# Permutation builds tied to a counted gather in the first pass of a two-layer graph network

## The reference

```python
def gcn_conv(x, edge_index, edge_weight, W, b, n_nodes):
    # self-loops added; norm = dinv[row] * ew * dinv[col]
    h = x @ W
    msg = h[row] * norm[:, None]
    out = segment_sum(msg, col, num_segments=n_nodes)
    return out + b

h = maximum(layernorm(x), 0)
x = x + log_softmax(gcn_conv(relu(gcn_conv(h, ..., W1, b1)), ..., W2, b2))
h = maximum(layernorm(x), 0)
msg  = relu(h[src] + edge_attr @ We + be)
aggr = segment_sum(msg, dst)
x = x + relu(batchnorm(relu((h + aggr) @ W1 + b1) @ W2 + b2))
```

## Time and profile before

| | us |
|---|---|
| median of 3 runs | 5606.34 |
| lowest and highest | 5599.08, 5607.18 |
| the profiled execution | 5616.2 |
| its span, first to last instruction | 5614.4 |
| TensorE busy | 4328.9 |
| VectorE busy | 3689.5 |
| GpSimd busy | 3768.6 |
| the first pass, first to last gather of the loop and its tail | about 270 to 2432 |

### The profile page before, as it was taken

One profiled execution on the slowest core, in us unless ns is written; L12 is line 12 of the kernel. 1 busy time (PEld: TensorE's weight loads), 2 busy tenths in 40 slices (PEclk: granted clock), 3 DMA queues, 4 the chain that ended last, 5 costly groups with the idle time before them and its releaser, 6 DMA issues.

```text
span 5614.4 us, 116632 instructions
## 1 busy us (share of the span) xinstructions
PE 4328.9 (77%) x29893; PEld 3358.6 (60%) x29894; DVE 3689.5 (66%) x10748; ACT 1292.0 (23%) x4287; POOL 3768.6 (67%) x3554
## 2 busy tenths in 40 slices
PE   4566666666666666668999999996699999999995
PEld 4444444444444444456777777775577777777773
DVE  3466666665666666647888888886666666666662
ACT  5111111111111111142111111113433333332223
POOL 2377777777777777737777777775666665666663
PEclk6577787777778787859999999996899999999997
DMA  2122222222222222212222222223232322222224
GB/s 54 37 47 46 50 47 47 48 47 48 46 48 46 49 48 49 46 52 52 52 51 51 51 51 51 51 48 111 65 70 65 70 68 66 70 62 67 63 59 109
DMA packets 239972, 316.92 MB, mean 56 GB/s; under 512 B 69263, under 2 KB 175178, under 8 KB 239545
## 3 DMA queue, kind: packets, MB, share of 16 engines
q0 software_dynamic: 111232, 170.85, 15.6%
q1 hardware_dynamic: 128688, 145.48, 8.9%
HBM read 276.92 MB, written 39.15 MB: 56 GB/s over the span
## 4 chain that ended last, share of the span: by engine, by line
PE 60%; DVE 13%; POOL 11%; issue 10%; DVEq 2%; ACT 2%; DMA 1%; POOLq 0%; ACTq 0%; SPq 0%
PE psum L1222 26%; PE psum L1142 15%; POOL rows_g L658 11%; PE psum L1165 7%; PE psum L1129 3%; DVE x_tab L1662 2%; PE psum L1086 2%; PE psum L1150 2%; PE psum L1154 1%; DVE x_tab L1657 1%; DVEq L432 1%; PE psum L1214 1%; PE psum L1289 1%; DMA rows_g<-table,idx 1%; DVE rows_g L1619 1%
## 5 line engine op out<-in xcount | busy, mean ns | idle before, releaser
L658 POOL DMA_INDIRECT rows_g<-table,idx x3476 | 3605.6, 1037 | 1547.3 <-issue 1011.3
L1222 PE MATMUL psum<-x_tab 125*128 x8512 | 1148.9, 289 | 83.9 <-issue 46.2
L1142 PE MATMUL psum<-hot,rows_g 128*96 128x128 f32 x7512 | 1077.4, 297 | 143.5 <-DMA rows_g<-table,idx 70.7
L1142 PEld LDWEIGHTS psum<-hot,rows_g 128*96 128x96 f32 x7512 | 980.8, 181 | 236.4 <-issue 145.8
L1222 PEld LDWEIGHTS psum<-x_tab 125*128 125x128 bf16 x8512 | 827.3, 97 | 393.9 <-issue 135.0
L1165 PE MATMUL psum<-x_tab 128*104 128x512 bf16 x2432 | 614.5, 403 | 534.4 <-DVE x_tab L1662 526.3
L1582 DVE TENSOR_TENSOR acc<-acc,psum 96x128 f32 x1173 | 328.8, 280 | 962.9 <-PE psum L1142 945.2
L791 ACT ACTIVATE attr<-edge 128x12 f32 (+1 forms) x1173 | 243.5, 211 | 2806.3 <-PE psum L1142 2805.6
L1165 PEld LDWEIGHTS psum<-x_tab 128*104 128x104 bf16 x2432 | 303.1, 133 | 780.6 <-ACT x_tab L848 321.9
L1573 DVE TENSOR_SCALAR hot<-iota,attr 128x128 f32<-128x128 f32 x2504 | 686.4, 356 | 7.3 <-ACT acc L785 4.8
L1619 DVE TENSOR_REDUCE rows_g<-psum 128x384 f32<-128x1152 f32 x304 | 412.3, 1356 | 341.2 <-PE psum L1222 336.9
(11 more groups left out here) (255 smaller groups left out, 3692.3 us busy)
## 6 DMA issues: line engine op xcount, KB each, us to landing
rows_g<-table,idx POOLq DMA_INDIRECT x3476, 2.5
x_tab<-sorted_keys SPq DMA_DIRECT2D x304, 125.0 KB
x_more<-in_edge_attr_dram SPq DMA_DIRECT2D x238, 64.0 KB
sorted_attr<-x_tab SPq DMA_DIRECT2D x38, 384.0 KB
x_more<-sorted_attr SPq DMA_DIRECT2D x152, 96.0 KB
table<-x_tab SPq DMA_DIRECT2D x13, 840.0 KB
x_tab<-in_edge_attr_dram SPq DMA_DIRECT2D x38, 256.0 KB, 2.8
x_tab<-in_x_dram SPq DMA_DIRECT2D x2, 4200.0 KB
```

What stands on the lines that cost most here:

```text
L658: pool.indirect_dma_start(out=rows_g[u][0:np_, g * F:(g + 1) * F], out_offset=None, in_=table[p], in_offset=bass.IndirectOffsetOnAxis(ap=i ...
L1142: last = pe.matmul(ps_agg[t.b], rows_g[t.u][0:t.np_, g * F:(g + 1) * F], hot[t.h][0:t.np_, g, :], start=g == 0, stop=g == G - 1)
L1222: last = pe.matmul(ps_sel[c], mask[i % 2][j][:, c * P:(c + 1) * P], tab3[:, j:J - KB + 1 + j, :, :][:, bass.ds(w[c], 1), :, :].rearrange(" ...
```

## The change

In the first pass GpSimd increments `fast.issue` ahead of every gather, so four times a step; in the other passes once a step, as before. Each build waits for that semaphore beside its old wait: build m of step k of iteration it waits for the count (it*U + k)*G + LEAD + m + 1 with LEAD = 16. In steps 3 to 7, those with three builds, VectorE's list is written in another order: build, addition, one hot, build, two hots, build, one hot. For that `build_hot` takes the columns that it is to build. Step 2 keeps its order and gets the wait.

```diff
+    LEAD = 16
...
             def gather(ring, p, s, u, np_, got):
                 pool.wait_ge(ring.staged, p * NS + s + 1)
-                pool.sem_inc(ring.issue, 1)
                 for g in range(G):
+                    if g == 0 or p == 0 and ring is fast:
+                        pool.sem_inc(ring.issue, 1)
                     pool.indirect_dma_start(
...
-            def build_hot(p, t):
+            def build_hot(p, t, columns=range(G)):
                 n = p * NS + t.s
                 np_ = t.np_
-                dve.wait_ge(fast.staged, n + 1)
-                dve.wait_ge(fast.agg, n + 1 + U - H)
+                if columns[0] == 0:
+                    dve.wait_ge(fast.staged, n + 1)
+                    dve.wait_ge(fast.agg, n + 1 + U - H)
...
-                    for g in range(G):
+                    for g in columns:
...
-                last.then_inc(fast.hot, 1)
+                if columns[-1] == G - 1:
+                    last.then_inc(fast.hot, 1)
...
-            def sort_perm(it, c):
+            def sort_perm(it, c, k, m):
                 dve.wait_ge(s_permd, SC * it + c + 1)
+                dve.wait_ge(fast.issue, (it * U + k) * G + LEAD + m + 1)
                 dve.tensor_scalar(perm[c % 3], iota_h, rank[:, c:c + 1], None, ALU.is_equal).then_inc(s_perm, 1)
...
+                        cs = PERM_AT.get(k, ())
+                        if len(cs) == 3:
+                            sort_perm(it, cs[0], k, 0)
+                            add_window(0, Step(it, k), w[k] * AL)
+                            build_hot(0, Step(it, k + LA), (0,))
+                            sort_perm(it, cs[1], k, 1)
+                            build_hot(0, Step(it, k + LA), (1, 2))
+                            sort_perm(it, cs[2], k, 2)
+                            build_hot(0, Step(it, k + LA), (3,))
+                            continue
                         build_hot(0, Step(it, k + LA))
...
-                        for c in PERM_AT.get(k, ()):
-                            sort_perm(it, c)
+                        for c in cs:
+                            sort_perm(it, c, k, 0)
```

## The result

The changed kernel takes 5660.07 us (median of 4 runs, 5658.26 to 5663.74), the kernel before 5605.26 us in the same comparison (5599.08 to 5607.18). The ratio is 1.0097 with a 95% interval from 1.0078 to 1.0116: slower by 54.8 us. The forecast was 5644 with a range of 5555 to 5705. The profiled execution of the changed kernel took 5663.74 us, 47.5 more than the profiled one of before.

A forecast was written before the change was run, and what follows sets the result against it. GpSimd's gathers were taken to bound the first pass. Stalls of 5.5 + 0.3 us an iteration against 4.8 gave +1.0, over 38 iterations +38 us on 5606: 5644 us, range 5555 to 5705.

The forecast's parts named there:

- What bounds the pass: First pass: it lasts as long as GpSimd's gathers; mean gather to rise from 1.076 to about 1.10 us, gap unchanged at 0.30.
- Signals and the wait: First pass: three more semaphore increments a step cost nothing; builds reach their waits 3.5 to 7.6 us late, so none holds.
- Rival B: First pass: waits hold, each build starts 0.2 us ahead of a gather, stretching it to 1.38 us; +80 us, 5686; chance 0.10.
- rival C: First pass: waits hold, but builds end before a gather's needs and stalls vanish; about -100 us, 5506; chance 0.03.
- The size: First pass: stalls beside builds go from 4.8 us an iteration to 5.5 + 0.3, so +1.0 us, +38 us over 38 iterations.
- The walk: Gathers followed through one step of the new order: three stalls, 0.24, 0.55 and 0.30 us, 1.09 a step, 5.5 an iteration.
- What it put at 0.55 us: GpSimd, let in at build 2's end, stops again inside build 3, which ends 1.17 us after build 2: 0.55 us lost.
- what it put at 0.30: GpSimd stops again in the next step's build 1, which ends 0.92 us after build 3: 0.30 us lost.
- the first hit: Build 2 nearly always hits a gather's stop, holding it for 0.27 us on average: 0.24 us a step.
- my upper bound of +3.6: Two hots and a build hold GpSimd as one, as three builds do: 8.4 us an iteration against 4.8, +3.6.
- The two stops: A long VectorE instruction can hold a gather at two points only, 0.13 and 0.79 us into it.
- The step of additions: First pass: the time from one VectorE addition to the next falls from 4.82 to 4.6 us.

The follow-up runs named there:

- `LEAD` 28: The changed kernel with LEAD = 28 in place of 16, so each signal comes three steps later; 5629.99 us, ratio 1.0026 to the kernel before.

## Why the prediction was right, and where it was not

*What bounds the pass.* Right. The idle time of GpSimd stayed at 475 us and all that moved was the mean gather, forecast at about 1.10 and measured at 1.104 us. Passes 2 and 3 kept their length within 0.4 us.

*Signals and the wait.* Right. The signals cost nothing, and the order alone gives the ratio of the whole change (1.0081 against 1.0097, overlapping). The builds come late to their signals, by 5 to 12 us in the mean and never by less than 2.7; I had worked out 3.5 to 7.6. That a signal runs twelve gathers ahead is confirmed by `LEAD` 28, with which waits begin to hold. Rival B's price of an aligned build (gather of 1.38 us) was met within 0.04 us there; rival C's shield didn't appear.

*The size.* The forecast was +1.0 us an iteration, and the stalls went from 5.27 to 6.34 us (mean of iterations 3 to 38), +1.07. Over 38 iterations that is 41 of the 42 us in the pass. The last 5 us of the profiled difference were in no term, and the medians differ by 7 us more than the profiled executions do.

*The walk.* Its mechanism stands: GpSimd slips in at the end of a build with a hot behind it and stops again inside the next build. What it put at 0.55 us (the next build 1.17 behind) is 2.12 - 0.94 - 0.63 = 0.55 in the gathers of 2.1 us (0.63 is the wait for build 2, from 0.13 us on), if they were let in at that build's end; what it put at 0.30 (0.92 behind) is 0.22 to 0.23. Two of its terms were mis-sized, and they cancelled. It took five of the 0.55 and four of the 0.30 an iteration, and the trace has 2.0 and 2.9. It took 0.24 us for the first hit, a mean over all phases, and the gathers that are stopped twice had waited 0.63 and 0.48 us at their first stop. So the sum of +1.0 came out by luck in part. The walk also spread the three stalls over gathers of 1.2 to 1.6 us. But first and second stop belong to one gather, so they add up in it: 165 gathers of 1.6 to 2.2 us carry 160 of the 248.8 us, 4.2 of 6.5 us an iteration, and those of 1.2 to 1.6 became fewer (176 to 146). That two hots and a build hold GpSimd as one, the mechanism of my upper bound of +3.6, is neither shown nor excluded; at every step it doesn't happen. Gathers over 2.4 us, which were to tell of it, are gone but for one of 2.98.

*The two stops.* I put them at 0.13 and 0.79 us into a gather, counted back from its end. That takes for granted that a release costs nothing. In the run with two builds ahead of the hots, 33 gathers met a build that stood behind an addition and began between 0.014 us before and 0.015 us after them, and none was held; all 125 that met such a build begun 0.018 us or more before them were. So what decides the first stop is whether a build runs on VectorE as the gather starts, or a hot with a build chained behind it (the 75 builds behind a hot began 0.003 to 0.026 us after the gather and held it). At the second, in the kernels without the further wait, builds behind an addition begun up to 0.534 us into a gather stopped it and none begun from 0.555 us on did, so it isn't at 0.79. Two figures do hold: a gather ends 0.82 us behind the release from its first stop and 0.12 behind that from its second. A build that ends less than 0.70 us behind the first release therefore costs nothing at the second stop, which is why builds 0.66 us apart are nearly free.

*The step of additions.* Forecast 4.6 us, measured 4.53.

*What I did not see.* The earlier trace rows has two groups of three builds of which one costs 1.61 us and the other 0.07 each for two gathers. I took the difference for phase alone. Part of it is, but at one and the same phase the kernel before has both outcomes (32 and 43), and one more met wait on the builds removes the dear one. The change carries that wait on every build, so it had a gain of its own, 37 us when run without the new order. The new order leaves one pair of builds in a row per iteration (steps 2 and 3), and even with the order alone, without the waits, that pair held no gather past its first build, so the gain had nothing to act on. The Trainium skill (SBUF — State Buffer, "Who interferes with whom") says the holder keeps the shared pair for its whole instruction. The traces agree for a single build; that a chain of three can hold GpSimd as one (2.56 us) is beyond what it states.

## What to carry to other kernels

Where GpSimd's gathers set the pace, look at two things on VectorE, not at the length of one instruction. One is the handover between long instructions: a group of three builds may cost 0.1 us or 1.6. The other is how far apart their ends are: where they follow each other by 0.66 us, a gather let in at one end loses nothing at the next; at 0.92 or 1.17 us it is stopped twice. Before tying such work to a count by signals, run the order alone and the waits alone: here they had opposite signs, +0.8% and -0.7%, and the fastest kernel took the order with the first build ahead and a wait that is always met, 5572.41 us against 5615.67. And a semaphore that GpSimd raises ahead of an indirect gather is raised here as the gather twelve places earlier begins, so that a wait on it may never hold anything.

## What the hardware showed that I had not expected

- A further wait on a VectorE build, though met long before, changes when a gather gets in: behind an addition, 0 of 461 gathers stopped in a build at their second stop were held past its end in the seven kernels of the table with it, against 59 of 96 and 7 of 83 without. The build itself isn't longer (three in 2.07 us in both). In the program the further wait puts one more instruction of VectorE's sequencer (21 ns in the trace) between two builds; whether that, or the wait as such, makes the opening isn't settled. The same kernels show a second difference: behind an addition, builds begun 0.48 to 0.54 us into a gather stopped it 46 times of 46 without the further wait and 0 times of 67 with it. A wait on a hot did nothing of the kind (stalls of 237.8 us with it).
- A gather asks for what VectorE holds in its first hundredths of a microsecond, and again some half a microsecond later: behind an addition, a build that began up to 0.014 us before a gather or up to 0.015 us after it let it pass (33 of 33, in 0.94 us), one begun 0.018 us or more before it did not (125 of 125).
- On one chip the kernel before took 24% longer, while an undisturbed gather took 0.944 to 0.947 us there too. In the traces of the four kernels that ran there 13 to 15% of the chain that ended last is put down to another core or an unknown queue, and GpSimd waited 298 us for staging in the first pass of the kernel with the first build ahead and counted waits, which waits for nothing on the usual chip. The second and third pass are longer there too (1830 to 1839 and 1998 to 2003 us, where the usual chips take about 1327 and 1557). What delayed the staging there is open.
